# Two states in one GpSimd operation: a state-space layer beside an fp8 feed-forward, on one core

## The reference, cut to what matters

```
dt  = softplus(dt_in @ Wdt + bdt)                # per channel and position
dA  = exp(A * dt)                                # per channel, state, position
dBu = (dt * B) * hs                              # the same
h   = dA * h + dBu ;  y = sum over the states of h * C
y   = (y + hs * D) * silu(gate) ;  out = y @ Wout
```

## Time and profile before

| | value |
|---|---|
| median of three runs | 1105.25 us |
| profiled execution | 1106.67 us |
| its span | 1104.6 us |
| VectorE busy | 1040.0 us (94%) |
| GpSimd busy | 921.1 us (83%) |
| TensorE busy | 933.1 us (84%) |
| ScalarE busy | 799.7 us (72%) |

### The profile page before, as it was taken

How to read it: one execution, slowest core, us unless ns; L and a number is a source line. 1 busy time by engine, 2 the same in 40 slices (tenths; PEclk the granted TensorE clock), 3 DMA queues, 4 the chain that set the end, 5 groups by cost and what they waited for, 6 DMA issues and landing times.

```text
span 1104.6 us, 14678 instructions
## 1 busy us (share of the span) xinstructions
PE 933.1 (84%) x4318; PEld 574.0 (52%) x4328; DVE 1040.0 (94%) x1222; ACT 799.7 (72%) x1134; POOL 921.1 (83%) x744
## 2 busy tenths in 40 slices
PE   3988899787778997888889979887998798869998
PEld 3756566344544554555445555544555555445554
DVE  7979888799999999999999999999999999999996
ACT  3877887677778665878786668787866687878662
POOL 4344425799898999989899999898999998989994
PEclk9999999878888998999989989999899899989999
DMA  7687878991111218332112193321211922212101
GB/s 278 200 275 223 306 223 317 364 370 58 51 56 38 85 40 307 122 133 77 58 40 76 68 319 106 110 77 58 76 49 67 352 96 77 77 58 77 39 1 39
DMA packets 53158, 150.24 MB, mean 136 GB/s; under 512 B 5729, under 2 KB 14049, under 8 KB 50017
## 3 DMA queue, kind: packets, MB, share of 16 engines
q1 hardware_dynamic: 53088, 149.41, 38.5%
HBM read 111.37 MB, written 38.01 MB: 135 GB/s over the span
## 4 chain that ended last, share of the span: by engine, by line
POOL 51%; issue 16%; DVE 16%; PE 8%; ACT 7%; DMA 1%; SPq 0%; DVEq 0%; POOLq 0%
POOL dbu L1034 34%; POOL hp L1052 12%; DVE prod L1064 4%; DVE da L1089 3%; DVE hp L1089 3%; POOL dt_du L371 3%; DVE gate_bf L1102 2%; DVE act L1105 2%; ACT gate_bf L966 2%; POOL hs_lo L366 1%; ACT da L988 1%; ACT L967 1%; ACT L966 1%; PE proj L600 1%; PE proj L599 1%
## 5 line engine op out<-in xcount | busy, mean ns | idle before, releaser
L988 ACT ACTIVATE da<-unit,neg_a 128x512 f32<-128x512 f32 x512 | 339.9, 684 | 216.4 <-DVE prod L1064 214.8
L1034 POOL TENSOR_TENSOR dbu<-unit,b_head 128x512 f32<-128x512 f32 x379 | 472.9, 1287 | 0.0
L1089 DVE TENSOR_TENSOR_SCAN da<-da,dbu 128x512 f32<-128x512 f32 x360 | 427.6, 1215 | 2.5 <-POOL dbu L1034 0.5
L1216 PE MATMUL yT<-ident,prod 128*128 128x128 f32 x1440 | 236.2, 294 | 113.4 <-DVE prod L1064 112.9
L1216 PEld LDWEIGHTS yT<-ident,prod 128*128 128x128 f32 x1440 | 177.4, 149 | 247.8 <-DVE prod L1064 200.9
L1052 POOL TENSOR_TENSOR hp<-hp,c_head 128x512 f32<-128x512 f32 x120 | 154.1, 1284 | 54.9 <-DVE act L1105 45.6
L1089 DVE TENSOR_TENSOR_SCAN hp<-da,dbu 128x512 f32<-128x512 f32 x152 | 183.5, 1207 | 8.3 <-ACT da L988 8.3
L1064 DVE TENSOR_TENSOR prod<-da,c_head 128x512 f32<-128x512 f32 x264 | 176.0, 667 | 0.0
L1034 POOL TENSOR_TENSOR dbu<-unit,b_all 128x512 f32<-128x512 f32 x128 | 160.6, 1285 | 0.0
L1165 PE MATMUL mm<-xn_b,w_sb 128*128 128x512 fp8e4 x512 | 150.4, 426 | 9.5 <-ACT gate_bf L998 6.6
L1177 PE MATMUL mm<-xnT_b,wgate 128*128 128x512 f32 x256 | 133.3, 614 | 0.9 <-ACT gate_bf L998 0.6
(11 more groups left out here) (118 smaller groups left out, 1280.5 us busy)
## 6 DMA issues: line engine op xcount, KB each, us to landing
unit<-unit_d SPq DMA_DIRECT2D x32, 768.0 KB, 4.3
unit_d<-dt_du SPq DMA_DIRECT2D x32, 512.0 KB, 2.7
wf<-in_wffn SPq DMA_DIRECT2D x12, 1024.0 KB, 6.4
c_head<-bc_d SPq DMA_DIRECT2D x24, 512.0 KB, 5.6
b_head<-bc_d SPq DMA_DIRECT2D x18, 512.0 KB, 4.9
unit_d<-hs SPq DMA_DIRECT2D x32, 256.0 KB, 6.5
w_sb<-w_d SPq DMA_DIRECT2D x64, 128.0 KB, 4.4
wgate<-in_win_gate SPq DMA_DIRECT2D x32, 256.0 KB, 2.7
```

The lines of the kernel that those rows point to most:

```text
L988: nc.scalar.activation(da[n % SLOTS][:, :], unit[:, k % 2, 0, :], ACT.Exp, scale=neg_a[:, k, n:n + 1]).then_inc(da_ready, 1)
L1034: nc.gpsimd.tensor_tensor(dbu[:, n % DBUS, :], unit[:, k % 2, 1, :], b_all[n // NS][:, n % NS, :], ALU.mult).then_inc(dbu_ready, 1)
L1089: nc.vector.tensor_tensor_scan(state, da[n % SLOTS][:, :], dbu[:, n % DBUS, :], 0.0, ALU.mult, ALU.add).then_inc(scanned, 1)
L1216: ins = nc.tensor.matmul(yT[k % 2][:, t * P:(t + 1) * P], product[:, t * P:(t + 1) * P], ident[:, :], start=False, stop=last, is_transpose ...
```

## The change

Three constants change. All eight units of a batch take the list FIVE. EARLY becomes 6. GpSimd makes the dbu of states n and n + 1 in one operation of 128 x 1024, at even n: its first input is the unit's `dt * hs` tile read twice (a broadcast over the two states), its second the group of two B tiles, its output two neighbouring dbu tiles. It waits until both tiles are free, and adds 2 to `dbu_ready` when it ends. The products with C stay at the same steps n.

```diff
-POOLED = (FIVE, FOUR, FIVE, FOUR, FIVE, FIVE, FIVE, FIVE)
+POOLED = (FIVE,) * KU
-EARLY = 5
+EARLY = 6
...
+        def two_states(slot, n):
+
+            twice = unit[:, slot, 1:2, :].broadcast_to([P, NS, L])
+            return nc.gpsimd.tensor_tensor(dbu[:, n % DBUS:n % DBUS + NS, :], twice, b_all[n // NS], ALU.mult)
+
         def head_start(pool):
...
             for n in range(EARLY):
-                nc.gpsimd.tensor_tensor(dbu[:, n % DBUS, :], unit[:, 0, 1, :], b_all[n // NS][:, n % NS, :], ALU.mult).then_inc(dbu_ready, 1)
+                if n % NS == 0:
+                    two_states(0, n).then_inc(dbu_ready, NS)
...
                 if not (opening and k == 0 and n < DBUS):
-                    pool.wait_ge(scanned, u * N + n - DBUS + 1)
-                nc.gpsimd.tensor_tensor(dbu[:, n % DBUS, :], unit[:, k % 2, 1, :], b_all[n // NS][:, n % NS, :], ALU.mult).then_inc(dbu_ready, 1)
+                    pool.wait_ge(scanned, u * N + n + NS - DBUS)
+                two_states(k % 2, n).then_inc(dbu_ready, NS)
...
-                    if not (opening and k == 0 and n < EARLY):
+                    if n % NS == 0 and not (opening and k == 0 and n < EARLY):
                         make_dbu(b, k, n, opening)
```

## The result

The changed kernel takes 1091.57 us (median of four runs, 1090.11 to 1093.36) against 1105.62 in the same runs for the kernel before. The ratio is 0.9866, 95% interval [0.9853, 0.988]: 14 us faster, where 14.3 were forecast. The profiled execution took 1091.34 with a span of 1089.6.

A forecast was written before the change was run, and what follows sets the result against it. VectorE bounds the scan stage, plus what a late GpSimd costs it. Gains of 6.60, 4.36, 1.72 and 1.65 us in units 1, 3, 7 and 0 sum to 14.3, from 1105.25 to 1090.9 us; range 1088 to 1099.

The forecast's parts named there:

- The cost of the pair: GpSimd: time from one two-state operation to the next, put at 2.32 us from opening rows, bounds 2.0 and 2.51.
- Units 6, 7 and 0: Scan-stage units without gate product: 7 and 0 become 25.26 us like unit 6, gaining 0.43 and 0.55 each.
- Rival C: Scan stage: another engine, TensorE, holds what GpSimd lets go; 1095 us, or 1098 if unit 1 keeps all; chance 0.08.
- Units 1 to 5: Scan-stage units with gate product, each then 0.95 us: unit 1 gains 1.76, unit 3 1.09, units 2, 4, 5 nothing.
- The wait of 0.39 for ScalarE: Unit 1, scan 1: a 0.38 us wait for ScalarE's `da`, hidden by GpSimd's lateness, was deducted from the gain.
- 6.60 + 4.36 + 1.65: Forecast gains in us over the whole run: unit 1 6.60, unit 3 4.36, unit 0 1.65.
- Unit 5: Scan stage, fifth gate-product unit of a batch: gain put at 0, length 28.5 us.
- The tail: After the last unit, with a 3.86 us wait for TensorE: 0.4 us less gain if it does not follow.
- The opening: GpSimd's head start before the first scan: three pairs end at 211.4, before `dt` at 211.84; cost 0.
- The microsecond of contention: Opening: five dbu took 7.16 us against 6.1, so about 1 us was contention, added to three pairs' 7.0.
- The price above the turning point: Scan stage: above 2.39 us per pair GpSimd bounds every unit; each further 0.01 costs 2.5 us in 32 units.
- cover for a late first pair: Next unit's first states: 0.3 us of slack, plus scan 1's 0.38 wait for ScalarE; cost 0.

The follow-up runs named there:

- e9: Changed kernel plus six one-column GpSimd clears behind every pair of the scan stage; 1116.52 us, ratio 1.009 to the kernel before.
- e1: Changed kernel with the old product lists (four products on GpSimd in units 1 and 3 of a batch); 1096.61 us, ratio 0.9921 to the kernel before.
- e7: Changed kernel without GpSimd's wait for act before its product of state 4; 1150.82 us, ratio 1.0397 to the kernel before.

## Why the prediction was right

*The cost of the pair.* 2.32 forecast from the slope between unlike rows, 2.32 measured. That the slope came out right was luck. The three rows don't lie on one line: from 256 to 512 columns it is 0.38 us more, for the next 512 it is 1.26. A line through the measured 1.23 and 2.32 gives 0.69 for 256 columns, an estimate. So the 256-column row (0.87) was too long by 0.18 and the 1024-column row (2.51) by 0.19, and the difference between them lost both. The trace shows what the two have in common: one of VectorE's casts ends 0.32 us after the start of each. The two casts merged in the earlier trace rows took 1.32 and 2.48 us, not 1.9 each. All twelve profiled runs have the same 2.50 to 2.53 there with such a cast, none has the row without one, so that contention is the likely cause and not a shown one. Taken as it stood, the row would have given a slower kernel, and e9 shows by how much.

*Units 6, 7 and 0.* 25.26 forecast; 25.27, 25.26 and 25.27. Rival C is out: TensorE is busy 26.60 of unit 1's 27.50 us, and VectorE doesn't wait for it.

*Units 1 to 5.* 27.50 and 28.54 forecast, 27.50 and 28.48 measured, with 0.53 us of room for 0.55. The wait of 0.39 for ScalarE did come back in unit 1 (the scan at 460.70), as it stands in unit 2 above (488.20). Over the 31 units the forecast terms are 6.60 + 4.36 + 1.65 and three times 0.43 in unit 7, 13.9 in all; measured 14.0. Unit 5 gave 0.04 to 0.07 us each time, put at 0: its gate product went from 1.27 to 1.29 down to 1.22.

*The tail.* I left open whether the last unit's 0.43 would reach the end. It did not. From that unit's first scan to the end are 38.7 us before and after, since the last `y` waits for TensorE, 3.86 us in the earlier trace rows and now 4.07:

```profile
1080.86 0.69 DVE L1078 TENSOR_TENSOR y<-yT,sg 128x512 f32<-128x512 f32 x1 [4.07 <-PE yT L1127]
```

*The opening.* The first scan came at 220.38 instead of 221.43, and so the profiled execution gained 1 us that no step claims. It lies within scatter: over the eight runs that have the changed kernel's stage A the first scan stands between 220.00 and 223.69. The microsecond of contention that I gave the head start is scatter too. Three pairs took 6.99 us in the changed kernel and 7.97 in e1. What I took for a property of the place was the clip of the weights (L466) happening to overlap it; in the changed kernel it overlapped the operation before, which took 1.94 us instead of 1.27.

*The price above the turning point* was my worst number. I had 2.5 us for each 0.01 of c, so 7 us at 2.42 and 32 at 2.52; it was 3.7 and 23.6. Units 6, 7 and 0 pay it in full, but 1 to 4 lost 0.07 at 2.42. VectorE's wait for ScalarE shrinks by what GpSimd delays it, from 9.5 us in all to 2.9 at 2.42 (it was counted as cover for a late first pair and then left out of the price), and a gate product has 0.13 us of lateness free.

## What to carry to other kernels

Where two engines share work in a loop, work out the length at which each would bound it, and the room at every place where they meet; then an edit's worth is a matter of hundredths of a microsecond per operation, and a filler of known cost finds the turning point directly. Before hiding one wait, look at which engine is next: the same edit (feed-forward matmuls and copies one state earlier) gave 4.4 us with GpSimd late and 9.7 with GpSimd in time. A price read from a row that ran beside a contending instruction is a bound and not an estimate. A slope between two such rows is right only if both are too long by the same amount, so look whether a third row lies on the line before you trust it.

## What the runs showed of the hardware

A 128x1024 f32 product with one input broadcast over two halves advances GpSimd by 2.32 us, a 128x512 by 1.23. One clear of 128x1 behind such a product adds 0.04 us, three add 0.11 and six 0.20, although each shows 105 to 109 ns in the records. A bf16 gate product or an fp8 clip on VectorE and an f32 product on GpSimd exclude each other for whole instructions: whichever comes second ends its own bare time, less 0.13 us, after the first (0.82 for 0.95, and 2.22 for a pair's 2.35 in e7). In the earlier trace rows, though, the gate product had to let two GpSimd instructions pass (one ended at 471.47, 0.53 us after it had begun, the next at 472.69). In e7 it had begun 0.85 us before the operation beside it ended at 484.10, and got in ahead of the next; what decides this was not tried.
